# 88 edge tiles summed by 0/1 matrices instead of 64 in a graph-layer kernel, with the gates multiplied into the matrices, a column buffer of 101 blocks that is used twice, and three lists of unequal length

## What is computed

```python
src, tgt = (x[row], x[col])                  # row = src, col = dst
h = relu(concatenate([src, tgt, edge_attr]) @ W1 + b1)
msg = h @ W2 + b2
attn_weight = sigmoid(concatenate([msg, conf]) @ Wa + ba)
out = segment_sum(msg * attn_weight, col, num_segments=N)
x = layernorm(x + out)
```

## Time and profile before

| | us |
|---|---|
| median of three runs | 632.19 |
| lowest, highest | 630.57, 634.38 |
| the profiled execution: span from first to last instruction | 633.1 |
| busy in it: PE / DVE / ACT / POOL | 389.8 / 471.5 / 425.3 / 461.5 |
| its 16 DMA engines, mean busy share | 0.76 |

### The profile page before, as it was taken

How to read it: one execution, slowest core, us unless ns; L and a number is a source line. 1 busy time by engine, 2 the same in 40 slices (tenths; PEclk the granted TensorE clock), 3 DMA queues, 4 the chain that set the end, 5 groups by cost and what they waited for, 6 DMA issues and landing times. The chain is left out here.

```text
span 633.1 us, 7692 instructions
## 1 busy us (share of the span) xinstructions
PE 389.8 (62%) x1737; PEld 262.0 (41%) x1737; DVE 471.5 (74%) x1561; ACT 425.3 (67%) x1089; POOL 461.5 (73%) x473
## 2 busy tenths in 40 slices
PE   1685887754755868385384868486767677587100
PEld 0453644443533545153352545354445454355100
DVE  6899988899794987857589869979778758274200
ACT  0257899879784996677367968877984979347100
POOL 7777775777177777777777767777777777777772
PEclk9988999787795869889598989696897789698555
DMA  6978788998986988959768998999899768633210
GB/s 160 356 223 284 262 305 280 333 322 264 329 297 211 322 276 307 319 162 309 252 234 291 311 305 277 305 363 324 279 335 311 212 223 226 185 93 88 63 50 15
DMA packets 84529, 159.29 MB, mean 252 GB/s; under 512 B 14018, under 2 KB 54278, under 8 KB 84482
## 3 DMA queue, kind: packets, MB, share of 16 engines
q1 hardware_dynamic: 69762, 129.47, 60.3%
q0 software_dynamic: 14720, 29.32, 16.0%
HBM read 99.75 MB, written 59.95 MB: 252 GB/s over the span
## 5 line engine op out<-in xcount | busy, mean ns | idle before, releaser
L791 ACT ACTIVATE nodes<-nodes,sc 128x128 f32<-128x128 f32 (+1 forms) x462 | 184.0, 486 | 0.0
L694 POOL DMA_INDIRECT out<-stash,row_idx x132 | 136.5, 1034 | 53.1 <-issue 39.9
L677 POOL DMA_INDIRECT rows_src<-x,src_list x132 | 134.3, 1018 | 40.9 <-issue 38.4
L919 PE MATMUL hid_ps<-turned,w 128*128 128x512 f32 x294 | 157.6, 677 | 4.4 <-ACT turned L772 4.3
L686 POOL DMA_INDIRECT rows_dst<-x,dst_list x132 | 127.5, 966 | 43.9 <-issue 39.6
L1191 DVE BATCH_NORM_STATS2 stats<-nodes 128x6 f32<-128x256 f32 (+1 forms) x358 | 133.6, 419 | 14.1 <-DMA nodes<-x 14.0
L772 ACT ACTIVATE turned<-turn_ps 128x512 f32<-128x512 f32 x147 | 79.9, 589 | 92.3 <-PE turn_ps L893 45.7
L929 PE MATMUL msg_ps<-w2x,hid 128*128 128x129 f32 x392 | 72.0, 342 | 60.2 <-ACT hid L777 60.2
L929 PEld LDWEIGHTS msg_ps<-w2x,hid 128*128 128x128 f32 x392 | 64.2, 248 | 65.9 <-ACT hid L777 65.9
L919 PEld LDWEIGHTS hid_ps<-turned,w 128*128 128x128 f32 x294 | 61.8, 226 | 67.6 <-issue 58.9
L677 POOL DMA_INDIRECT rows_src<-x,src_near x64 | 61.2, 957 | 21.2 <-issue 18.9
(11 more groups left out here) (129 smaller groups left out, 514.5 us busy)
## 6 DMA issues: line engine op xcount, KB each, us to landing
nodes<-x SPq DMA_DIRECT2D x62, 704.0 KB, 6.8
out<-nodes SPq DMA_DIRECT2D x62, 704.0 KB, 4.8
attr_in<-edge_attr SPq DMA_DIRECT2D x49, 256.0 KB, 6.4
near_dst<-line SPq DMA_DIRECT2D x16, 256.0 KB, 7.1
near_x<-x SPq DMA_DIRECT2D x20, 192.0 KB
near_x<-x SPq DMA_DIRECT2D x24, 128.0 KB
near<-x SPq DMA_DIRECT2D x4, 704.0 KB
out<-near SPq DMA_DIRECT2D x4, 704.0 KB, 7.6
```

Of the source, the lines that this page charges most:

```text
L677: pool.indirect_dma_start(out=rows_src[:, k % RING, j, :], out_offset=None, in_=x[:, :], in_offset=bass.IndirectOffsetOnAxis(ap=idx[:, j:j ...
L694: pool.indirect_dma_start(out=out[:, :], out_offset=bass.IndirectOffsetOnAxis(ap=column(row_idx, i, j), axis=0), in_=stash[:, list_slot(i) ...
L791: return act.activation(row, row, ACT.Identity, scale=sc[0:parts, b % 2, 0, col:col + 1], bias=sc[0:parts, b % 2, 1, col:col + 1])
L919: last = pe.matmul(hid_ps[:], w1[:, c, :], turned[:, k % 2, c, :], start=(c == 0), stop=(c == 2))
```

## The change

- The near part grows from 64 tiles over 91 blocks to 88 tiles over 168 blocks (22 steps); the lists shrink from 33 groups to 27, in lists of 9, 11 and 7 groups. The 49 steps stay. Windows are now up to 5 blocks wide; those of 5 are summed in two pieces (3 and 2 blocks, `PARTS`).
- The gates are multiplied into `place` by the same instruction that makes it (`ALU.is_equal, ALU.mult` with `weight`); ACT no longer scales the messages of near steps. So `make_place` moves from the step before into `sum_near`, one call for each tile, two tiles ahead of the sum.
- The column buffer `near` holds 101 blocks (`HELD`): blocks 80 to 167 lie in it first, and after their rows are out, blocks 0 to 66 use the same columns. 13 blocks are copied (`move_near`), and 67 cleared in three pieces (`clear_near`, at steps 24, 31, 36).
- Rows of the near blocks go through the chunks' ring of six slots as units of 11 blocks (16 units, still in 512-byte pieces); 56 chunks are left. `NEAR_AT` says which batch has one. Of a unit's three pieces of `turn_sums`, PE does two before `turn(k+1)` and one behind it.
- `SCATTERS` puts a scatter of one group into nearly every near step from 13 on; 7 groups are left for the end, where 11 were.
- `ACT_ROWS` is 8, 8, 8. `turned` and `hid` have one buffer instead of two.

```diff
-DT = 64
+DT = 88
-LT = 44
+LIST_GROUPS = (9, 11, 7)
-NB = 91
+NB = 168
-KG = (1, 1, 1, 1, 2, 2, 2, 2, 2, 2, 3, 3, 3, 3, 3, 4)
+KG = (1, 1, 1, 1, 2, 2, 2, 2, 2, 2, 3, 3, 3, 3, 3, 4, 4, 4, 4, 4, 5, 5)
+PARTS = {1: ((0, 1),), 2: ((0, 2),), 3: ((0, 3),), 4: ((0, 4),), 5: ((0, 3), (3, 5))}
+CLEARED = {24: (42, 67), 31: (18, 42), 36: (0, 18)}
-LIST_CHUNKS = (15, 39, 63)
+LIST_CHUNKS = (15, 39, 56)
+NEAR_STEPS = (2, 5, 13, 16, 19, 21, 23, 26, 28, 30, 32, 34, 36, 38, 40, 41, 43, 44, 45, 46, 47, 48)
-            48: tuple(range(22, 33))}
+            45: (18,), 46: (19,), 48: tuple(range(20, 27))}
-ACT_ROWS = (7, 7, 8)
+ACT_ROWS = (8, 8, 8)
...
@@ gpsimd: which stores a list's first scatter waits for
-                    if i in (0, 11, 22):
-
+                    if first_of_list(i):
+                        rows_end = UNIT_OF_CHUNK[LIST_CHUNKS[list_of(i)] - 1]
                         for u in range(SLOTS):
-                            pool.wait_ge(stored[u], 16 * len(range(u, LIST_CHUNKS[i // LG], SLOTS)))
+                            pool.wait_ge(stored[u], 16 * uses_up_to(u, rows_end))
                     if i == 0:
                         pool.wait_ge(list_ready, 2)
-                        pool.wait_ge(near_stored[0], 16)
...
@@ scalar, gates(k)
                 act.activation(weight[:, k % 2], logit[:, k % 2], ACT.Sigmoid).then_inc(weight_ready, 1)
+                if is_near(k):
+                    return
...
@@ tensor, sum_near(k)
-                pe.wait_ge(place_ready, n + 1)
+                pe.wait_ge(raw_ready, k + 1)
                 for j in range(G):
-                    use = USE[(D_, n, j)]
-                    bank_free(use)
-                    pe.wait_ge(gated_ready, G * k + j + 1)
+                    pe.wait_ge(place_ready, G * n + j + 1)
                     b = first + j * width
-                    pe.matmul(sum_ps[:, use % 2, 0:width * P], gated[:, k % 2, j, :], place[:, b * P:(b + width) * P],
-                              start=True, stop=True).then_inc(sum_ready, 1)
+                    for h, (low, high) in enumerate(near_parts(n)):
+                        use = USE[(D_, n, j, h)]
+                        bank_free(use)
+                        pe.matmul(sum_ps[:, use % 2, 0:(high - low) * P], gated[:, k % 2, j, :],
+                                  place[:, (b + low) * P:(b + high) * P], start=True, stop=True).then_inc(sum_ready, 1)
...
@@ tensor, main loop
-                for piece in row_pieces_at(k):
+                for piece in row_pieces_at(k)[:2]:
                     turn_sums(*piece)
                 if k + 1 < K:
                     turn(k + 1)
+                for piece in row_pieces_at(k)[2:]:
+                    turn_sums(*piece)
...
@@ vector
+            def make_place(k, j):
+                g = STEPS[k][1]
+                n, width = near_number(g), KG[g]
+                t, b = g * G + j, half_of(n) + j * width
+                dve.tensor_scalar(place[:, b * P:(b + width) * P], iota[:, 0:width * P], in_block[:, t:t + 1],
+                                  weight[:, k % 2, j:j + 1], ALU.is_equal, ALU.mult).then_inc(place_ready, 1)
...
+                dve.wait_ge(weight_ready, k + 1)
+                make_place(k, 0)
+                make_place(k, 1)
                 for j in range(G):
...
+                    if j + 2 < G:
+                        make_place(k, j + 2)
+                    for h, (low, high) in enumerate(parts):
+                        use = USE[(D_, n, j, h)]
+                        dve.wait_ge(sum_ready, use + 1)
+                        wait(dve, near_added, adds_before(n) + j * len(parts) + h)
+                        window = near[:, low * P:][:, bass.ds(bases[j], (high - low) * P)]
+                        dve.tensor_tensor(window, window, sum_ps[:, use % 2, 0:(high - low) * P], ALU.add
+                                          ).then_inc(near_added, 1)
```

More of the change, by code:

```diff
@@ L108, in before_in_buffer, with near_parts, adds_before, units_in_order @@
     return n if alone else n - 1
[L112 to L119, removed]
+def near_parts(n):
+    return PARTS[KG[DG - 1 - n]]
+def adds_before(n):
+    return sum(G * len(near_parts(m)) for m in range(n))
+def units_in_order():
+    units, chunk = [], 0
+    for b in range(BATCHES):
+        for i in range(TRIO):
+            if (b, i) in NEAR_AT:
+                units.append((D_, NEAR_AT[b, i]))
+            elif b <= LAST_CHUNKS_IN:
+                units.append((S_, chunk))
+                chunk += 1
+            else:
+                units.append(None)
+    return units
+UNITS = units_in_order()
+CHUNKS = sum(u is not None and u[0] == S_ for u in UNITS)
+UNIT_OF_CHUNK = {u[1]: c for c, u in enumerate(UNITS) if u is not None and u[0] == S_}
+NEAR_UNIT = {u[1]: c for c, u in enumerate(UNITS) if u is not None and u[0] == D_}
+def use_of_slot(c):
+    return sum(UNITS[d] is not None for d in range(c % SLOTS, c, SLOTS))
+def uses_up_to(u, c):
+    return sum(UNITS[d] is not None for d in range(u, c + 1, SLOTS))
+def unit_rows(c):
+    kind, of = UNITS[c]
+    return NEAR_ROWS[of][1] - NEAR_ROWS[of][0] if kind == D_ else ROWS
+def is_chunk(c):
+    return c is not None and UNITS[c][0] == S_
+def chunk_of_batch(b, i):
+    c = TRIO * b + i
+    return c if 0 <= c < len(UNITS) and UNITS[c] is not None else None
+def near_of_batch(b):
+    for i in range(TRIO):
+        if (b, i) in NEAR_AT:
+            return i, NEAR_AT[b, i]
+    return None
+def act_rows(c):
+    return min(ACT_ROWS[c % TRIO], unit_rows(c) - 1)
+def row_pieces(q):
+    low, high = NEAR_ROWS[q]
+    return [(q, first, min(first + 4, high)) for first in range(low, high, 4)]
 def row_pieces_at(k):
-    return [p for b in NEAR_BATCHES for p in row_pieces(b).get(k, ())]
-ADDED_BEFORE = {b: sum(top > low for top in FINAL.values()) for b, (low, _) in NEAR_OUT.items()}
+    return [p for (b, i), q in NEAR_AT.items() if min(2 * b, K) == k for p in row_pieces(q)]
+ADDED_BEFORE = [sum(top > low for top in FINAL) for low, _ in NEAR_ROWS]
 def sum_uses():
@@ L149 @@
 PIECES = [u[1:] for u in USES if u[0] == "rows"]
-def taken_before(first, last):
-    return max((i + 1 for i, (_, low, high) in enumerate(PIECES) if low < last and high > first), default=0)
 def list_groups_of(b):
@@ L167, in crosses @@
 def crosses(b):
-    return 3 * b + 2 < 62
+    c = TRIO * b + 1
+    return all(is_chunk(chunk_of_batch(b, i)) and UNITS[c + i - 1][1] < CHUNKS - 1 for i in (1, 2))
 def node_column(b, i, r):
-    before = 0 if i == 0 else even(ROWS) + (i - 1) * (ROWS if crosses(b) else even(ROWS))
-    return COLS[b]["nodes"] + before + r
+    return COLS[b]["unit", i] + r
 def columns(b):
     at, n = {}, 0
-    if 3 * b < 63:
-        at["nodes"] = n
-        n += even(ROWS) + (2 * ROWS if crosses(b) else 2 * even(ROWS))
+    for i in range(TRIO):
+        c = chunk_of_batch(b, i)
+        if c is not None:
+            at["unit", i] = n
+            n += ROWS if i and crosses(b) else even(unit_rows(c))
     for i in list_groups_of(b):
@@ L1092, in _ @@
             columns_of = {}
-            for width in range(1, 5):
+            for width in range(1, MOST + 1):
                 for w in range(width):
@@ L1125, in _ @@
             step(dve.tensor_reduce(flags[0:1, 0:1], c[1], AX_X, ALU.add))
+            step(dve.tensor_reduce(flags[0:1, 6:7], below, AX_X, ALU.add))
             dve.wait_ge(consts_in, 16 * 8)
```

443 lines of the change are left out of this document (221 added, 222 removed).

## The result

The changed kernel takes 658.95 us (median of 4 runs, 658.6 to 660.45), the kernel before beside it 632.48 (630.57 to 634.38): ratio 1.0413, 95% interval 1.0377 to 1.0449. Slower by 4%, where 3% faster was forecast. Once more, beside other runs, it took 660.1 against 633.4 (1.0402, 1.0349 to 1.0455). The profiled execution took 658.92 us, with a span of 657.1. I go by the span: 614 was forecast, 657.1 came, 43 more.

A forecast was written before the change was run, and what follows sets the result against it. POOL's indexed DMAs were taken as the bound, with DVE close under it. Step 12 at 170, steps 13 to 48 in 413 to 583, then the final scatters and closing to a span of 614: forecast 613 us, range 596 to 636.

The forecast's parts named there:

- POOL bounds the kernel before: POOL's 460 indexed DMAs set the end of the kernel before; 24 gathers and 24 scatters go, 62 us.
- DVE's added work, +41: DVE over the whole kernel: 41 us more busy time, about 6 before step 12 and 35 behind.
- To step 12: 170: Start to step 12's bias addition: 160 becomes 170 us, 6 of DVE's work and 4 of new handshakes.
- The first scatter: POOL reaches its first scatter at 137 us, stalls 32 for stores landing at 169; DVE idles about 9 at step 14's gathers.
- Steps 13 to 48: 413: Steps 13 to 48 take 413 us, 359 of DVE busy and 54 idle, ending at 583.
- Gates: DVE's idle time for gates in steps 13 to 48: 4 us, as near steps no longer wait for scaled messages.
- messages: DVE's idle time for PE's messages in steps 13 to 48: 7 us, PE being ahead again.
- The end: T + 31: After the steps end (T, 583): 28 final scatters from 566 to 602, then 11.7 us of closing, 614.
- Rival 3: Near steps: DVE and PE handshakes cost 3 us each in 20 steps, not 0.8; 44 us more, 657; 12%.
- Rival 2: Transfers bind: 17 batches each wait 1.5 us for chunks, 20 us more, 633, no change; 9%.
- Rival 1: DVE follows POOL's pace: idle time behind step 12 falls, steps end at 564, total 590 to 603 us; 21%.
- The port rule: DVE scalar operations and POOL instructions exclude each other: 88 matrices each wait up to 0.96 us, some 60, 674 us; 2%.

The follow-up runs named there:

- matrices a step early: Changed kernel with place made without gates one step early and ACT scaling the near messages again: 778.9 us, ratio 1.0064.
- Turning first: Changed kernel with PE turning the rows of step k+1 ahead of the near sums of step k-1: 644.6 us, ratio 1.016.

## Why the prediction was wrong, point by point

- *POOL bounds the kernel before; the change takes that away.* Right, and shown: 588 us without its scatters; after the change POOL waits for PE. (Its "12.3 us a step" behind step 12 is 11.8 by the earlier trace rows, 424 us over 36 steps; nothing rests on it.)
- *DVE's added work, +41.* Measured +51. Of the 10 us too few, 5.7 are in steps 13 to 48 (364.7, not 359). Near additions, pick, rows and list work came within 2 us each. Place was mis-sized, +18 and not +11 (groups of L1412: 37.9 us in all, 19.6 before). The second operation, with its operand from a tile, makes each dearer: the widest of the earlier trace rows took 477 ns, this kernel's own 20 of that width without gates, in the run of matrices a step early, 483, and gated
```profile
L1412 DVE TENSOR_SCALAR place<-iota,in_block,weight 128x512 f32<-128x512 f32 x20 | 10.4, 564 | 1.1 <-ACT weight L838 1.1
```
- *To step 12: 170.* 172.8. Right within 3.
- *The first scatter: stores landed at 169, gathers of step 14 near 187, DVE idle 9.* Right: the scatter starts at 169.57, PE turns step 14 from 182.3 to 188.6, DVE idles 10.5 us. The stall is 19.6 us and not 32, as POOL came at 150 and not at 137: it waits for PE's turnings already.
- *Steps 13 to 48: 413.* **This step failed**: 460.4. Of the 47 us, 6 are work and 42 idle time. By its items: stall 10.5 (9), near sums 10.8 (16), third piece 9.2 (8), chunks under 1.6 (10): right or too high. **Gates: 30.3, where "4, half of 8.3" stood, and messages: 26.0 without the stall, where "7, for PE is ahead again" stood.** These two are 45 us short; 9 us more are short waits outside the list above. The working looked at what DVE waits for inside the near step, and found it small, rightly. It did not ask what stands behind the near sums on PE: turn(k+1), then ACT's copies, its eight rows and its gates. A wait of PE that costs DVE nothing in its own step costs it twice in the next. The sentence that PE's added work (47 us in the stretch, 283.7 to 330.8) is "covered unless DVE waits for it inside a step" was the error. Turning first, which changes only the order on PE, gives most of messages and gates back (36.5 to 7.4, 21.0 to 6.6); with the first scatter later too, the idle time is 63.4 us. Apart from the stall that is 18 us above the forecast's 45, where the changed kernel was 40 above. What is left is mostly near sums (40.6, not 16), and why they cost so much behind the turning was not tested.
- *The end: T + 31.* T + 24: final scatters start 25 us before the steps' end, not 17. 7 us too much.
- 3 + 47 - 7 = 43, the whole error.
- *Rival 3, slower, 657.* Its number (657.1 came) and its point (from 75 us idle on; 95.7 came) are met, and so is its clause that the messages stand behind it all on PE. It put the price in the wrong place: the handshake for near sums costs 10.8 us, under the mark of 50 that was to show it. Turning first showed the true place. That the number agrees to the us is luck. At 12% its chance was too low: that the sums stand before the turning and the matrices inside the step was plain from the code.
- *Rival 2, transfers*: false, no chunk waits left. *Rival 1*: false.
- *The port rule* of the Trainium skill (SBUF — State Buffer, "Who interferes with whom"), 60 us: the 88 matrices take 37.9 us together; by the rule, as the prediction priced it, they would have taken some 60 us more. So DVE doesn't pay. But the prediction looked at DVE alone. On POOL's side the trace agrees with the rule that the later of two instructions is held. Most of POOL's 412 indexed DMAs take 0.94 to 0.95 us; of 20 that start while DVE makes a pick (two tensor inputs, not the scalar form of which the prediction spoke), 16 end 0.81 to 0.87 us after that pick, and one lasts 3.21 us. In step 34:
```profile
460.86 0.94 POOL L744 DMA_INDIRECT rows_dst<-x,dst_list  x1 [0.31 <-issue]
461.52 1.22 DVE L1451 TENSOR_TENSOR pick<-near_dst,node_of 128x1024 f32<-128x1024 int32 x1
462.10 1.45 POOL L744 DMA_INDIRECT rows_dst<-x,dst_list  x1 [0.30 <-issue]
```
Added up over the trace, POOL is busy 32 us longer than at 0.944 us a DMA, 18 of them behind picks and 3 behind place. In the kernel before it is 25 us, 10 of them behind picks. These 7 us more are most of the 10 by which POOL's busy time fell less than forecast. They cost the changed kernel little, since POOL no longer bounds it; in the kernel before, picks held the very engine that set the pace.

## What to carry to other kernels

When a change moves work of engine X into the stretch in which engine Y holds its queue for it, price it by what stands *behind* Y's waiting instruction and by who waits for that, around the whole loop. Taking the bound off one engine gives the time of the next loop, not of the next engine: run or work out the kernel without the old bound first (588 us here), and add the change to that. And such a loop may be cut by the order of two of its parts: independent work goes ahead of the work that must wait.

## What the runs showed that I had not expected

With turning first, relieving the busiest engine did nothing in steps 13 to 48: 21 us less of DVE's work, 1 us less time. With place gated, a 128x512 matrix takes 564 ns and not 477, 128x128 355 and not 299. POOL's indexed DMAs stretch by up to 2.3 us behind a pick of DVE. And one kernel, turning first, with nearly the same busy time of DVE took 644.6 us in one group of runs and 766.8 in another, where it was not 1.6% slower than the kernel before, but equal to it within the interval (0.9915 to 1.0023).
